# One gathered tile fewer a superunit, dense sums placed by a one-hot product, and moments and normalisation by matmul, in a graph layer

## The reference

```python
e = relu(_bn(edge_attr @ ee_w1 + ee_b1, ee_g1, ee_bb1)) @ ee_w2 + ee_b2
h = x + segment_sum(e, dst, N)
neigh = segment_sum(h[src], dst, N)
z = h + neigh
z = relu(_bn(z @ mlp_w1 + mlp_b1, mlp_g1, mlp_bb1))
z = relu(_bn(z @ mlp_w2 + mlp_b2, mlp_g2, mlp_bb2))
out = _layernorm(x + z)
```

## Time and profile before

| what | value |
|---|---|
| median of 3 runs | 2282.17 us (2281.79 to 2283.35) |
| profiled execution | 2281.99 us, span 2280.2 us |
| mean granted clock of PE | 0.961 |
| busy over the span | PE 2106.6 us (92%), DVE 1833.7 (80%), ACT 1000.2 (44%), POOL 1648.8 (72%) |
| moments and set-up | 0 to 100 us |
| edge sums | 100 to 632 us |
| h stage and preparation of the loop | 632 to 711 us |
| loop of 52 superunits | 711 to 2149.5 us |
| layers | 2149.5 to 2208 us |
| normalisation | 2208 to 2280 us |

### The profile page before, as it was taken

One profiled execution on the slowest core, in us unless ns is written; L12 is line 12 of the kernel. 1 busy time (PEld: TensorE's weight loads), 2 busy tenths in 40 slices (PEclk: granted clock), 3 DMA queues, 4 the chain that ended last, 5 costly groups with the idle time before them and its releaser, 6 DMA issues. The chain is left out here.

```text
span 2280.2 us, 57729 instructions
## 1 busy us (share of the span) xinstructions
PE 2106.6 (92%) x15974; PEld 1659.1 (73%) x15974; DVE 1833.7 (80%) x3770; ACT 1000.2 (44%) x1753; POOL 1648.8 (72%) x1645
## 2 busy tenths in 40 slices
PE   5699999999975999999999999999999999999873
PEld 5699999999943777777777777777777777777532
DVE  7799999999997777777777777777777777777578
ACT  0022222222253555555555555555545545555476
POOL 3188888888867777777777777777777777777213
PEclk7799999999997999999999999999999999999985
DMA  6433333333362211111111111111111111112015
GB/s 199 138 107 101 102 109 101 103 108 101 92 203 66 54 54 54 53 54 54 53 54 54 53 54 54 53 54 54 53 54 54 53 54 54 53 54 54 22 42 183
DMA packets 86254, 174.97 MB, mean 77 GB/s; under 512 B 36619, under 2 KB 38171, under 8 KB 85893
## 3 DMA queue, kind: packets, MB, share of 16 engines
q1 hardware_dynamic: 46086, 97.33, 14.1%
q0 software_dynamic: 36608, 75.05, 11.9%
q10 hardware_dynamic: 3407, 1.21, 0.3%
HBM read 160.67 MB, written 12.80 MB: 76 GB/s over the span
## 5 line engine op out<-in xcount | busy, mean ns | idle before, releaser
L805 POOL DMA_INDIRECT table<-h_scratch,idx x1144 | 1079.6, 944 | 353.9 <-issue 348.3
L934 DVE TENSOR_TENSOR table<-ps,keys 128x480 bf16<-128x480 f32 x1300 | 816.7, 653 | 14.1 <-PE ps L827 11.9
L840 PE MATMUL ps<-table,counts_even 128*128 128x384 bf16 x2600 | 530.2, 327 | 0.0
L840 PE MATMUL ps<-table 128*128 128x384 bf16 x2600 | 528.1, 326 | 0.0
L893 ACT CAST counts_even<-ps 128x480 bf16<-128x480 f32 x650 | 363.4, 559 | 366.4 <-PE ps L827 364.6
L893 ACT CAST table<-ps 128x480 bf16<-128x480 f32 x650 | 363.4, 559 | 351.2 <-PE ps L827 350.1
L827 PE MATMUL ps<-table 128*128 128x240 bf16 x2600 | 480.6, 267 | 27.5 <-DVE table L934 22.9
L585 PE MATMUL ps<-table 128*128 128x96 f32 x3328 | 414.5, 278 | 0.0
L585 PEld LDWEIGHTS ps<-table 128*128 128x128 f32 x3328 | 388.6, 192 | 0.0
L827 PEld LDWEIGHTS ps<-table 128*128 128x128 bf16 x2600 | 253.2, 101 | 183.0 <-DVE table L934 41.6
L852 PEld LDWEIGHTS ps<-table 128*128 128x128 f32 x2288 | 278.4, 192 | 59.9 <-issue 52.6
(11 more groups left out here) (151 smaller groups left out, 1399.5 us busy)
## 6 DMA issues: line engine op xcount, KB each, us to landing
table<-in_edges_t SPq DMA_DIRECT2D x416, 128.0 KB, 2.5
table<-h_scratch,idx POOLq DMA_INDIRECT x1144, 2.5
table<-in_edges SPq DMA_DIRECT2D x26, 512.0 KB, 4.5
table<-in_x_t SPq DMA_DIRECT2D x48, 256.0 KB, 2.9
h_scratch<-table SPq DMA_DIRECT2D x24, 256.0 KB, 2.0
out<-table SPq DMA_DIRECT2D x24, 256.0 KB, 2.0
table<-in_dst_groups SPq DMA_DIRECT2D x1, 832.0 KB
table<-in_dst_mixed SPq DMA_DIRECT2D x1, 832.0 KB
```

The costliest lines, as they stand in the source:

```text
L805: pool.indirect_dma_start(near_rows[:, u, t * D:(t + 1) * D], None, h_dram, bass.IndirectOffsetOnAxis(ap=idx[:, v, at + t:at + t + 1], axis=0)
L840: mm = pe.matmul(ps[:, PACK_BANKS[v], 0:SPLITS * D], counts[(v * LISTS + c) % 2][:, b, :], h_split[:, j * SPLITS * D:(j + 1) * SPLITS * D] ...
L934: dve.tensor_tensor(match[:, k], ps[:, 0, 0:LIST_COLS].unsqueeze(1).broadcast_to([P, 2, LIST_COLS]), keys[:, v, c, 2 * k:2 * k + 2].unsque ...
```

## The change

- **Loop.** 21 gathered tiles (6, 5, 5, 5) and 11 dense ones a superunit; a dense tile covers 11 destination nodes instead of 12. A list is 11 tiles of 220 columns, in six sets (five of two tiles, one of one), matched by three DVE instructions of four, four and three tiles. The bank rule is the same for every set.
- **Dense sums.** `placing` is a one-hot of 104 columns, made by DVE from the tiles' places; `fold` multiplies by it instead of by the identity, and one addition of 104 columns (`add_span`) takes the place of the ten additions.
- **Moments.** A column of ones stands beside each block of 128 columns in SBUF, so that the product also gives the column sums; each load is laid out in pieces of 128 columns with a stride of 129. DVE's sums and the `dst_groups` load go. All minima and maxima come from `dst_mixed` in 52 rows. PE's test for wide groups stands ahead of its last two loads; the preparation of `base`, `rel` and `place` stands ahead of DVE's wait for the last load. ACT's queue gets two more constants, a fourth transfer of bases and 11 small ones out, and 11 that bring the tiles' places back. The product that gives `per_edge` moves to the start of the h stage.
- **Normalisation.** PE multiplies by `center` (identity minus 1/128) in place of the transposes, so that the rows come out centred. ACT squares a chunk from PSUM, DVE sums the squares of the four rows, ACT takes the root with a scale of 1/128, DVE the reciprocal, and DVE multiplies the whole chunk in one instruction. The statistics, the shift and the normalising on ACT go.

```diff
-NARROW = 12
+NARROW = 11
+SPAN = 104
-GATHER = (6, 5, 6, 5)
-DENSE = 10
+GATHER = (6, 5, 5, 5)
+DENSE = 11
+SETS = (DENSE + 1) // 2
+MATCHES = ((0, 4), (4, 8), (8, DENSE))
+PACKS_AT = (0, 4, 8, 11, 14, 17, LIST)
...
                 def load(s, n):
-                    sp.dma_start(rows[:, s, 0:GRAM_COLS],
-                                 a["edges"][:, bass.ds(n * GRAM_COLS, GRAM_COLS)]).then_inc(gram_in[s], 16)
+                    sp.dma_start(gram_rows[:, s, :, 0:P],
+                                 a["edges"][:, bass.ds(n * GRAM_COLS, GRAM_COLS)].rearrange("p (b w) -> p b w", w=P)
+                                 ).then_inc(gram_in[s], 16)
                 def reload(s, i):
                     sp.wait_ge(gram_done, i * GRAM_SLOTS + (s + 1 - GRAM_SLOTS))
-                    sp.wait_ge(gram_summed, i * GRAM_SLOTS + (s + 1 - GRAM_SLOTS))
...
+                for t in range(DENSE):
+                    act.dma_start(turned_dram[t, :].rearrange("(r o) -> r o", o=1),
+                                  least_mixed[:, STREAMS + t:STREAMS + t + 1]).then_inc(base_out, 16)
...
-                        mm = pe.matmul(ps[:, 0, 0:P], x, x, start=(n == 0 and b == 0), stop=True,
-                                       skip_group_check=True)
+                        mm = pe.matmul(ps[:, 0, 0:P + 1], gram_rows[:, s, b, 0:P], gram_rows[:, s, b, :],
+                                       start=(n == 0 and b == 0), stop=True, skip_group_check=True)
...
+                pe.wait_ge(cleared, 2)
+                pe.wait_ge(spread, 3)
+                pe.matmul(ps[:, 6, 0:1], ones, wide[:, 0:1], start=True, stop=False)
+                pe.matmul(ps[:, 6, 0:1], ones, wide[:, 3:4], start=False, stop=True).then_inc(wide_ready, 1)
                 for s in range(GRAM_REST):
                     gram_slot(None, s, GRAM_BODIES)
...
         def bank_freed(s, p):
-            return s * LISTED + (0 if p == 0 else p - RING if p < RING else p - RING + 1)
+            return s * LISTED + (p - RING + 1)
...
-                        pe.matmul(ps[:, PACK_BANKS[v], SPLITS * D:(SPLITS + 1) * D], quarters, ident[:],
+                        pe.matmul(ps[:, PACK_BANKS[v], SPLITS * D:SPLITS * D + SPAN], quarters, placing,
                                   start=True, stop=True).then_inc(folded, 1)
...
+                    def match_list(s, v, c, m):
+                        first, last = MATCHES[m]
                         dve.wait_ge(keyed, s + 1)
-                        wait(dve, listed, s * LISTED + (c * PAIRS + k - PAIRS + 1))
-                        dve.tensor_tensor(match[:, k],
+                        wait(dve, listed, s * LISTED + (c * SETS + (last + 1) // 2 - SETS))
+                        dve.tensor_tensor(match[:, first:last, :],
...
+                    def add_span(s, v, windows):
+                        at = dve.value_load(base_i[0:1, bass.ds(s + NEAR_GROUPS, 1)], min_val=0, max_val=N)
                         dve.wait_ge(folded, s + 1)
                         dve.wait_ge(added, windows)
-                        wait(dve, dense_added, s * DENSE + t)
-                        here = table[:, 0, bass.ds(at, NARROW)]
+                        wait(dve, dense_added, s)
+                        here = table[:, 0, bass.ds(at, SPAN)]
...
                     def sum_splits(s, v):
+                        wait(dve, folded, s)
+                        dve.tensor_tensor(placing, ps[:, 0, 0:SPAN], place[:, bass.ds(s, 1)].broadcast_to([P, SPAN]),
+                                          ALU.is_equal)
                         dve.wait_ge(packed, (s + 1) * LISTS)
...
+                def center_rows(c, s, n):
                     pe.wait_ge(residual, c + 1)
-                    wait(pe, normed[s % 2], by_parity(c - BANKS, s))
-                    turn(pe, s, summed[:, s % 2, :], n).then_inc(turned2, 1)
+                    wait(pe, normed, c - (BANKS - 1))
+                    for k in range(PER):
+                        mm = pe.matmul(ps[0:n // PER, s, k * D:(k + 1) * D], summed[:, s % 2, k:n:PER], center[:],
+                                       start=True, stop=True)
+                    mm.then_inc(centered, 1)
...
+                def square(c, s, n):
+                    q = n // PER
+                    act.wait_ge(centered, c + 1)
+                    wait(act, measured, c - 3)
+                    act.activation(squares[0:q, s % 4, :], ps[0:q, s, :], ACT.Square).then_inc(squared, 1)
```

More of the change, by code:

```diff
@@ L62 @@
 GRAM_COLS, GRAM_SLOTS = 1024, 4
+GRAM_BLOCKS = GRAM_COLS // P
 GRAM_LOADS = TILES * ED // GRAM_COLS
@@ L337, in _ @@
[L337 to L346 removed]
+                dve.wait_ge(groups_in, 16)
@@ L360, in _ @@
-                dve.tensor_reduce(wide[0:HALVES, 3:4], most_mixed[:], AX_X, ALU.max).then_inc(spread, 1)
-                with dve.Fori(1, GRAM_BODIES) as i:
-                    for s in range(GRAM_SLOTS):
-                        sum_slot(s, i)
-                for s in range(GRAM_REST):
-                    sum_slot(s, GRAM_BODIES)
-                dve.wait_ge(gram_summed, GRAM_LOADS)
-                link(dve.tensor_reduce(part1, part.rearrange("p n c -> p c n"), AX_X, ALU.add))
+                dve.tensor_reduce(wide[0:MIXED, 0:1], most[:], AX_X, ALU.max)
@@ new lines, in _ @@
+                dve.wait_ge(base_in, 16)
+                dve.wait_ge(spread, 5)
+                dve.wait_ge(place_in, 16 * DENSE)
+                dve.wait_ge(weights_in, 16 * WEIGHTS)
+                dve.tensor_tensor(place[:], place[:], base[:, SPAN_AT:DENSE_AT], ALU.subtract).then_inc(spread, 1)
+                dve.wait_ge(spread, 6)
+                dve.tensor_scalar(place[:], place[:], wide[:, 2:3], place_col[:, 0:1], ALU.mult, ALU.add)
+                for first, last, width in ((SPAN_AT, BASES, NARROW), (GROUPS, SPAN_AT, NEAR), (0, GROUPS, WINDOW)):
+                    ins = dve.tensor_scalar(base[:, first:last], base[:, first:last], wide[:, 2:3], float(width),
+                                            ALU.mult, ALU.subtract)
@@ L880, in _ @@
                     body(MIXED_BODIES - 1, last=True)
-                    for k in range(PAIRS):
+                    for k in range(SETS):
                         pack(MIXED - 1, 1, LISTS - 1, k)
```

378 lines of the change are left out of this document (172 added, 206 removed).

## The result

The changed kernel takes 2198.52 us (median of 4 runs, 2194.66 to 2200.66) against 2281.98 (4 runs, 2281.55 to 2283.35): a ratio of 0.963, 95% interval 0.9618 to 0.9642. The forecast was 2185, with a range of 2160 to 2215. The profiled run took 2194.66 us with a span of 2192.5, and is the fastest of its four.

The account below looks back on a forecast made before the run. POOL's gathers were taken to pace the loop, with PE close behind. Loop, loop's end, moments, h stage and normalisation summed as 2282.0 - 53.6 - 7.5 - 25.6 + 1 - 12 = 2184.3, stated as 2185 us, range 2160 to 2215.

Parts of the forecast that it names:

- The loop: Loop of 52 units: one gather fewer and both PE stalls gone give 26.4 us a unit, 53.6 us less in all.
- The lower bound, POOL's 26.22: Loop: no unit faster than POOL's 21 gathers at 1.2484 us, 26.22 us, which would save 63 us.
- the sign that the gathers would no longer run back to back: Loop: with units about 26.4 us apart, PE would be the bound and POOL's gathers would show gaps.
- the slower rival: Loop: PE stands at every list for the first 880-column match, 260 us more, 2445 us; chance 0.03.
- The loop's end: After the last fold: nine of ten narrow additions go, 7.5 us less, bounds 6.5 to 8.
- The moments: First stage: loads no longer wait for DVE, moments end at 61, first one-hot at 74.5, 25.6 us earlier.
- The rival of loads that don't speed up: Moments: 512 B pieces or DVE's checks holding the `wide` matmuls end them near 76; 2200 us; chance 0.12.
- The sign that was to show it wrong: Moments: the forecast is wrong if the clock stays at the lower level because PE waits for loads.
- The extra transaction of unaligned pieces: Moments' loads: pieces starting off a 256 B boundary cost 17 beats for 16, some 4 us more, by estimate.
- The h stage: Stage after the edge sums: moved per-edge product and four subtractions for two, 1 us more.
- The normalisation: Last stage: four resources at 1.5 to 1.7 us with hand-overs give 1.85 us a chunk for 2.36, 12 us less.
- The tables: Normalisation rival: Square and Sqrt switch ACT's tables twice a chunk, 59 us more, 2244 us; chance 0.03.

Follow-up runs that it names:

- fewer: Kernel before the change, with 21 gathers a unit instead of 22 and the fourth tile's rows summed in place of the fifth's: 2240.81 us, ratio 0.9818.
- place: Changed kernel with the 22 small transfers replaced by a DVE copy and one PE product: 2191.6 us, ratio 0.96 to the kernel before.
- again: Changed kernel run once more as it is: 2199.76 us, ratio 0.9641 to the kernel before.
- pieces: Changed kernel with the ones column laid out in DRAM, so loads land in runs of 4128 B instead of 512 B pieces: 2189.87 us, ratio 0.9595.
- relu: `set` with ACT's normalisation relu writing strided into four contiguous blocks, so PE and POOL work on contiguous columns: 2180.12 us, ratio 0.954 to the kernel before.
- center2: Changed kernel with the second layer's product reading its moving columns strided, so everything behind it is contiguous: 2211.52 us, ratio 0.9688 to the kernel before.
- warm: Kernel before the change, with 54 unused PE products between the last fold and the layers: 2280.4 us, ratio 0.9991.
- center: Changed kernel with POOL's addition reading strided and writing four contiguous blocks, so PE's centring weights are contiguous: 2203.28 us, ratio 0.9657 to the kernel before.
- set: Changed kernel with the edits of `place`, `pieces` and `memset` together: 2185.84 us, ratio 0.9577 to the kernel before.
- all: Changed kernel with the edits of `place`, `pieces`, `memset` and `center` together: 2189.07 us, ratio 0.9587 to the kernel before.
- memset: Changed kernel with POOL's big memset waiting until DVE has finished its checks and cast: 2198.32 us, ratio 0.9632 to the kernel before.

## Why the prediction was right or wrong

**The loop: right in its mechanism, under by 7 us.** The gathers paced it, as `fewer` shows, and both stalls went. The term that was off is PE's unit, taken as 26.4 and measured as 26.20. The five phases are as reckoned, 4.29 each or 21.45. The four streams' sums and the fold take the other 4.75 us, where the 26.47 of the working implied 5.02. The working took PE's need out of a unit that waits. There five tiles took 1.14 us, and five that don't wait take 1.06 (1304.03 to 1305.09); and the wait was 0.67, not 0.51: four packs pass in 0.65 us elsewhere, and the last four before the wait began 1.32 ahead of the sums.

```profile
1334.41 0.81 PE L840 MATMUL ps<-table,counts_even 128*128 128x384 bf16 x4
1335.73 1.30 PE L852 MATMUL ps<-table 128*128 128x64 f32 x10 [0.51 <-DMA table<-h_scratch,idx]
```

The trace of the kernel before had PE's own pace in it. In its second and third unit, while the gathers are still ahead of PE, a unit takes 26.59 us (first lists of the second and the third unit):

```profile
739.54 0.36 PE L827 MATMUL ps<-table 128*128 128x240 bf16 x2
...
766.13 0.36 PE L827 MATMUL ps<-table 128*128 128x240 bf16 x2
```

That is the unit of `fewer`. Less the stall of 0.26 and the tile of 0.23, and 0.04 more for the lists, it gives 26.14. A unit of the middle of the loop is 1.23 us shorter (27.43 to 26.20) and not 1.03; over the stretch it is 60.8 / 52 = 1.17, since these early units of the kernel before were short already. The lower bound, POOL's 26.22, is where the unit came out, and the sign that the gathers would no longer run back to back did not come. Within the loop no list waits for a match, and the phases are 4.29 us, so the slower rival had no ground.

**The loop's end: right**, -7.3 for -7.5.

**The moments: wrong, and this is the step:** "Eleven tiny transfers out and eleven back on ACT's queue lie beside the loads; they are needed only by 60." They were costed at nothing because nothing waits for them early. But the loads suffer from them: both go through the same 16 DMA engines, which move half as much meanwhile. By the slices above, an estimate, 22 us at 136 GB/s instead of 279 lose 22 x (1 - 136/279) = 11.3 us. That counts all fifteen transfers out. What the runs show of the 22 that are new is `place`: its products end at 71.8, 5.4 us earlier than in the changed kernel and 7.3 earlier than in `again`, and its median is 8.2 us lower. The four transfers that are left there go with a shorter slow stretch (26.59 to 35.01, when `base` goes). The rate taken for pieces of 512 B was right: 277 forecast, 266 to 271 measured at full share. So 60 us for the bytes, 11.3 for the small transfers, 2 for the first slice in which nearly nothing lands, and some 3 from the last landing (between 72 and 74) to the end of the products make about 76. Measured are 77.2, and 79.1 in `again`. The chain behind was right as well: 13.5 forecast, 13.6 measured (77.2 to 90.82).

The rival of loads that don't speed up named 2200, and it is the one that came about, though for a reason that it did not name: neither the pieces, whose price the forecast held already, nor a held `wide` product, but the transfers of ACT. The sign that was to show it wrong did show: the clock at 0.63 while PE waits for loads.

"DMA: Bandwidth & Descriptors" of the Trainium skill (Specifications) says that a piece must be 512 B or more for the full rate, since a shorter one is read, modified and written. The pieces of the eleven transfers out have 4 B a row, those of the other four 4 to 44. The runs show their price; that it is this mechanism no run shows. The extra transaction of unaligned pieces, of which the prediction spoke from the same page, was not tried by itself: `pieces` changes length and alignment together, and what it gained, 308 GB/s at a share of 0.91 for 271 at 1.02, is a quarter per busy share, more than the one beat in sixteen of that estimate. The section tells of what a transaction reads, and these pieces lie off the boundary where they are written.

**The h stage: right**, +0.5 for +1; the preparation of the loop adds 0.8 that was not counted.

**The normalisation: right in size for a wrong reason.** 1.87 us a chunk for 1.85, and -10.5 for -12; that the sizes agree is luck. The sum laid four resources at 1.5 to 1.7 beside each other, with hand-overs; in fact PE alone is the bound, with eight steps of 0.233. The prediction took PE's price from the transposes, which read `summed` with the same stride of four (`k:n:PER`, L667) at a clock of 0.50, and put PE at 1.7 to 2.26 "at the lower clock". The 1.87 lies in that bracket, but from 2145 to 2180 the clock is 1.00. It is the stride that keeps the step at 0.233 there, where a contiguous one takes 0.112 (eight in 0.97 us in `relu`); at the lower clock the two hardly differ (eight in 1.78), so the rows of the kernel before couldn't show the stride's price. Nor were the other engines at 1.5 to 1.7: with PE freed and none of them burdened (`center2`), chunks come 1.37 us apart at their fastest, and the stage is 4.9 us shorter. In `relu` it is 2.7 us shorter only, because ACT's write became the bound.

**The tables: right.** Square runs 25 times, and ACT's one table load is still the only one:

```profile
12.05 1.28 ACT L255 ACT_TABLE_LOAD   x1 [12.05 <-issue]
```

The page "ScalarE: Activation LUTs" of the Trainium skill (Table sets: the hidden batching unit) does not name square among the functions of every set; here it needed no switch beside Relu and Sqrt.

**The layers: not foreseen, and luck.** -2.6 us, though their code is the same. PE stands 9.1 us idle ahead of them before, 1.8 after, and the clock at their start is 0.62 before, 1.00 after. `warm` raises the clock in the old kernel and gets 1.8 of the 2.6. So the clock explains most of the gain, but what sets it at that place is open, and it is not the idle time alone: `pieces` and `center` have the same 2.1 us between the last fold and the first product as the changed kernel, and yet a clock of 0.72 in the first 6 us, and their layers take 58.2 and 58.1. `place`, `set` and `all` are like them (57.9 to 58.1); `again` and `memset` keep the gain (56.1). In the profiled runs of `place`, `pieces` and `set` this loss of some 2 us stands against what the moments gained.

## What to carry to other kernels

Small transfers are not free because nobody waits for them: look at what else is in flight on the DMA engines while they are, and read GB/s beside the busy share, for the share alone (0.79 in that window) hides it. A strided operand is paid by whoever touches it with the stride, so give it to the engine with idle time, and cost it from a row with the same stride at the same clock. Take the price of a piece of work from a row that had not waited: here the first units of the kernel before had it.

## What the runs showed of the hardware

**Stride.** f32 with a stride of four cost PE and POOL, and a write that jumps 128 floats cost ACT: PE's step with a weight load 0.233 us for 0.112 at a clock of 1.00 (at 0.50, 0.233 for 0.213), PE's product of 512 moving columns 1078 ns for 617, POOL's addition of 512 2116 for 1270, ACT's relu of 512 1286 for 802. "SBUF — State Buffer" of the Trainium skill (Door 1: The DMA port swizzle) says that SBUF is read in lines of 16 bytes, that each access that goes to a new line pays, and that a stride of up to four f32 is free. Four floats are 16 bytes, a new line each time: the rows agree with the first part, with prices of 60 to 108% at full clock, and not with the second at a stride of exactly four.

**Cast beside memset.** A cast of 1664 columns took 11.27 us beside POOL's memset and 1.01 without. The two rows of the changed kernel:

```profile
36.31 10.61 POOL L287 MEMSET table<- 128x12608 f32 x1 [24.47 <-DVE most_mixed L348]
```

```profile
36.53 11.27 DVE L354 CAST rel<-table 128x1664 f32<-128x1664 int32 x1
```

The memset starts 0.22 us ahead and ends at 46.92; the cast ends at 47.80, 0.88 later, nearly the whole length of a cast alone. So it did not share, it stood. The same page (Who interferes with whom) says that a cast in one of DVE's two-port modes and a GpSimd instruction exclude each other, and that the first to start keeps the ports to its end, which is what these rows show. The kernel before has the same pair (memset 10.61 us from 27.78, cast 11.28 from 27.98), and there the loads did wait for the sums that stand behind the cast; no run moved that memset.

**Open.** Why transfers of 4 B a row on one queue make the packets of another take 55 ns for 32 was not tried further, nor what sets the clock at the layers' start.
